# Column halves for offsets and products, and VectorE's work spread over an image's chunks, in a two-stage convolution kernel

## The reference

```python
x = x + L0(_gn(x))      # 1x1 conv 64 -> 128 channels; a 3x3 depthwise convolution whose nine taps
                        # are computed per image from the pooled hidden units by two small layers;
                        # y * tanh(softplus(y)); 1x1 conv 128 -> 64
x = x + L1(_gn(x))      # deformable 3x3 convolution, below
```

```python
offset = _conv2d(x, w_off, b_off)                       # 18 channels
mask = sigmoid(_conv2d(x, w_mask, b_mask))              # 9 channels
val = bilinear samples of x at 9 shifted points per pixel (4 corners each), times mask
xd = einsum('bikhw,oik->bohw', val, w_def)
cat = concatenate([xd, offset, mask], axis=1)
z = einsum('bihw,oi->bohw', cat, w_1x1) + b_1x1         # then a batch norm with given statistics
return silu(z)
```

## Time and profile before

| | |
|---|---|
| time, median of 3 runs (lowest to highest) | 5764.49 us (5759.78 to 5768.8) |
| the profiled execution's own time | 5764.16 us |
| its span | 5762.4 us |
| granted TensorE clock, mean | 0.833 of full speed |
| busy: TensorE matmul | 4653.8 us (81%) |
| busy: VectorE | 4582.5 us (80%) |
| busy: GpSimd | 4105.2 us (71%) |
| busy: ScalarE | 2165.7 us (38%) |
| gathers issued by GpSimd | 4308 |

### The profile page before, as it was taken

The page is one execution under the profiler, slowest core; times in us unless marked ns, Lnnn a source line. Parts: engine busy times, 40 slices in busy tenths (PEclk is TensorE's granted clock), DMA queues, the critical chain, the costliest instruction groups (busy, mean ns, idle before and its releaser), DMA issues.

```text
span 5762.4 us, 38546 instructions
## 1 busy us (share of the span) xinstructions
PE 4653.8 (81%) x11780; PEld 1745.7 (30%) x11780; DVE 4582.5 (80%) x5064; ACT 2165.7 (38%) x3057; POOL 4105.2 (71%) x4315
## 2 busy tenths in 40 slices
PE   7576888978879788787887878788897887988783
PEld 3122332323323233232332323233232332323231
DVE  5978969789696886969879697886978979688664
ACT  3333434343343433434434344343433434343320
POOL 1777677776767767677776777767777677776776
PEclk8777888978789787888988889788887888978895
DMA  3334353343534435344343443434334353433433
GB/s 97 106 121 132 99 139 109 117 131 104 142 95 131 122 106 138 94 132 118 111 136 94 132 117 114 134 98 139 109 116 130 97 146 101 129 114 106 123 108 101
DMA packets 281823, 675.11 MB, mean 117 GB/s; under 512 B 77119, under 2 KB 116618, under 8 KB 279370
## 3 DMA queue, kind: packets, MB, share of 16 engines
q0 software_dynamic: 206784, 564.93, 33.2%
q1 hardware_dynamic: 74832, 107.71, 7.4%
HBM read 618.23 MB, written 54.12 MB: 117 GB/s over the span
## 4 chain that ended last, share of the span: by engine, by line
PE 57%; DVE 28%; POOL 6%; issue 5%; ACT 2%; DMA 1%; POOLq 0%; DVEq 0%; ACTq 0%; SPq 0%
PE yo_ps L733 15%; PE z_ps L672 8%; PE conv_ps L630 7%; DVE pairs L1280 6%; DVE conv_ps L1171 6%; POOL gat L493 6%; DVE gat L1301 6%; PE yo_ps L630 5%; PE tap_ps L663 4%; PE z_ps L739 4%; PE conv_ps L553 3%; PE z_ps L671 3%; PE xh_ps L638 2%; DVE stat L1197 1%; DVE xb L1195 1%
## 5 line engine op out<-in xcount | busy, mean ns | idle before, releaser
L493 POOL DMA_INDIRECT gat<-patch_table,ixu x4308 | 4097.2, 951 | 1643.5 <-issue 1268.0
L1301 DVE TENSOR_TENSOR gat<-gat,wgt_ps 128x1024 f32<-128x1024 f32 x1077 | 1305.1, 1214 | 553.4 <-DMA gat<-patch_table,ixu 546.6
L733 PE MATMUL yo_ps<-hat_s,hat_image 128*128 128x512 f32 x3000 | 1398.0, 614 | 8.7 <-DVE hat_wy L1335 8.7
L1280 DVE TENSOR_REDUCE pairs<-gat 128x256 f32<-128x1024 f32 x1024 | 1240.2, 1211 | 0.0
L663 PE MATMUL tap_ps<-ident,pairs 128*128 128x128 f32 x2048 | 398.2, 326 | 838.1 <-DVE pairs L1280 838.1
L973 ACT ACTIVATE val<-tap_ps 128x512 f32<-128x512 f32 x512 | 304.6, 595 | 1439.2 <-PE tap_ps L663 1438.2
L733 PEld LDWEIGHTS yo_ps<-hat_s,hat_image 128*128 128x128 f32 x3000 | 562.5, 196 | 821.2 <-issue 734.5
L672 PE MATMUL z_ps<-val,w_pair 128*64 128x512 f32 x1024 | 668.0, 752 | 13.6 <-ACT val L973 13.6
L663 PEld LDWEIGHTS tap_ps<-ident,pairs 128*128 128x128 f32 x2048 | 262.1, 162 | 1217.9 <-DVE pairs L1280 1033.8
L1171 DVE SCALAR_TENSOR_TENSOR conv_ps<-xh,kb,conv_ps 128x1024 f32<-128x1024 f32 x480 | 617.8, 1287 | 12.7
L1335 DVE TENSOR_TENSOR hat_wy<-yo_ps,hat_wy 128x512 f32<-128x512 f32 x300 | 206.6, 689 | 250.7 <-PE yo_ps L733 248.0
(11 more groups left out here) (219 smaller groups left out, 4304.9 us busy)
## 6 DMA issues: line engine op xcount, KB each, us to landing
gat<-patch_table,ixu POOLq DMA_INDIRECT x4308, 2.7
xb<-in_x SPq DMA_DIRECT2D x31, 1024.0 KB, 9.7
patch_table<-rec SPq DMA_DIRECT2D x120, 256.0 KB, 2.3
hat_image<-patch_table SPq DMA_DIRECT2D x135, 128.0 KB, 4.6
out<-n_z SPq DMA_DIRECT2D x128, 128.0 KB
patch_table<-np SPq DMA_DIRECT2D x2, 1072.5 KB
patch_table<-gat SPq DMA_DIRECT2D x8, 256.0 KB, 2.2
patch_table<-rec SPq DMA_DIRECT2D x16, 97.0 KB
```

What stands on the lines that cost most here:

```text
L493: pool.indirect_dma_start(gat[:, k, t * 2 * REC:(t + 1) * 2 * REC], None, table_rows, bass.IndirectOffsetOnAxis(ixu[:, i, k, t:t + 1], 0)) ...
L733: m = pe.matmul(hat_sum[:, :], hat_image[:, i, t, :], hat_s[:, i, :], start=(i == 0), stop=(i == HI - 1))
L1280: dve.tensor_reduce(total, gat[:, k, :].rearrange("p (t x c h) -> p t c x h", t=TILES, x=2, h=2), mybir.AxisListType.XY, ALU.add).then_inc ...
L1301: dve.tensor_tensor(patch, patch, wk.rearrange("p (n h) -> p n h", h=2).unsqueeze(2).to_broadcast([128, TILES * 2, C, 2]), ALU.mult).then_ ...
```

## The change

- `has_hat`: chunks 3 and 4 of image 0 also compute their ninth tap; images 1 to 15 keep chunks 0 to 4. The table rows for it are also loaded for image 0 (`load_hat_image(0)`).
- `to_z`: every product into `z_ps` becomes two matmuls of 256 columns, the first half into partitions 0 to 63, the second into 64 to 127 of the same 256 columns of PSUM. SiLU becomes two instructions.
- `offsets_two`: the offsets of two chunks go into `om_ps`, one into partitions 0 to 40, the other into 64 to 104, alternating.
- The clip at 20 leaves VectorE: ScalarE computes relu(20 - y) and then exp(20 - that).
- `normalise` of the upper copy and the normalisation of the input in `hidden` go to ScalarE.
- `x_stats` moves from chunks 0 to 3 to chunks 5 and 6; `x_mean`, `x_var`, `x_norm`, `hidden_units`, `kernel_taps`, `kernels` from chunk 4 to chunk 7; `points` is done in two halves, for chunks 0 to 3 during chunk 6 and for chunks 4 to 7 during chunk 7; `hidden` runs at units 6 to 9 of chunk 7 instead of 4 to 7.
- `hat_post 0` moves from unit 2 to unit 3. Statistics, last row and pixels use the banks `om_ps`, `tr_ps` and `yo_ps` instead of `xh_ps`, with the waits that this asks for.

```diff
+HATS0 = (3, 4)
 HATS = (0, 1, 2, 3, 4)
-NH = len(HATS)
...
-PLAN_FIRST = ((2, "convolve 0"), (3, "convolve 1"), (5, "convolve 2"), (6, "exp"), (7, "ln"), (7, "x_stats"), (8, "tanh"))
+PLAN_FIRST = ((2, "convolve 0"), (3, "convolve 1"), (5, "convolve 2"), (6, "exp"), (7, "ln"), (8, "tanh"))
 PLAN_BLOCK0 = ((1, "project"), (3, "residual"), (3, "convolve 0"), (4, "convolve 1"), (5, "convolve 2"), (6, "exp"),
-               (7, "ln"), (7, "x_stats"), (8, "tanh"), (8, "finish"))
+               (7, "ln"), (8, "tanh"), (8, "finish"))
 PLAN_START = (
     ((2, "convolve 0"), (3, "convolve 1"), (3, "first_offsets 2"), (5, "first_offsets 3"), (5, "convolve 2"), (6, "first_pixels 1"), (6, "exp"),
-     (6, "first_offsets 4"), (7, "ln"), (7, "x_stats"), (7, "first_points 2"), (8, "tanh"), (8, "first_offsets 5"), (KK, "first_pixels 2")),
+     (6, "first_offsets 4"), (7, "ln"), (7, "first_points 2"), (8, "tanh"), (8, "first_offsets 5"), (KK, "first_pixels 2")),
     ((1, "project"), (3, "residual"), (3, "convolve 0"), (3, "first_offsets 6"), (4, "convolve 1"), (4, "first_offsets 7"), (5, "first_pixels 3"),
-     (5, "convolve 2"), (6, "exp"), (6, "first_points 3"), (7, "ln"), (7, "x_stats"), (8, "tanh"), (8, "finish")),
+     (5, "convolve 2"), (6, "exp"), (6, "first_points 3"), (7, "ln"), (8, "tanh"), (8, "finish")),
     ((1, "project"), (3, "residual"), (3, "convolve 0"), (4, "convolve 1"), (5, "convolve 2"), (6, "exp"), (6, "first_points 4"),
-     (7, "ln"), (7, "x_stats"), (8, "tanh"), (8, "finish")),
+     (7, "ln"), (8, "tanh"), (8, "finish")),
 )
-PLAN_NORM = ((1, "project"), (3, "residual"), (4, "x_mean"), (4, "group_mean"), (5, "x_var"), (6, "group_var"), (6, "x_norm"),
-             (7, "hidden_units"), (8, "kernel_taps"), (8, "finish"), (8, "normalise"), (KK, "kernels"))
+PLAN_NORM = ((1, "project"), (3, "residual"), (4, "group_mean"), (5, "group_var"), (6, "normalise"), (8, "finish"))
 PLAN_PREPARE = (
-    ((1, "last_row"), (1, "to_table 0"), (2, "offsets 0"), (3, "to_table 1"), (3, "offsets 1"),
-     (4, "to_table 2"), (5, "to_pixels 0"), (5, "to_table 3"), (6, "offsets 2"),
-     (7, "offsets 3"), (8, "to_table 4"), (8, "finish"), (KK, "to_pixels 1")),
-    ((1, "offsets 4"), (2, "offsets 5"), (2, "to_table 5"), (3, "to_pixels 2"), (4, "offsets 6"), (4, "to_table 6"),
-     (5, "offsets 7"), (6, "to_table 7"), (7, "to_pixels 3"), (8, "finish")),
-    ((1, "points 0"), (2, "points 1"), (2, "next_indices"), (3, "points 2"), (4, "hidden 0"), (5, "hidden 1"),
-     (6, "hidden 2"), (7, "hidden 3"), (8, "finish")),
+    ((1, "last_row"), (1, "offsets 0"), (2, "to_table 0"), (2, "x_stats 0"), (3, "to_table 1"), (4, "offsets 1"), (4, "to_pixels 0"),
+     (5, "to_table 2"), (5, "x_stats 1"), (6, "to_table 3"), (7, "to_pixels 1"), (8, "to_table 4"), (8, "finish")),
+    ((1, "offsets 2"), (2, "to_table 5"), (2, "points 0"), (3, "offsets 3"), (3, "to_pixels 2"), (4, "points 1"), (4, "to_table 6"),
+     (5, "x_stats 2"), (5, "to_table 7"), (6, "points 2"), (6, "to_pixels 3"), (7, "x_stats 3"), (8, "finish")),
+    ((1, "x_mean"), (1, "points 3"), (2, "x_var"), (2, "points 4"), (2, "next_indices"), (3, "x_norm"), (3, "points 5"),
+     (4, "hidden_units"), (5, "kernel_taps"), (6, "kernels"), (6, "hidden 0"), (7, "hidden 1"), (8, "hidden 2"), (8, "finish"), (KK, "hidden 3")),
 )
-PLAN_HAT = ((1, "hat_rows"), (1, "hat_up 0"), (2, "hat_post 0"), (3, "hat_up 1"), (5, "hat_post 1"), (5, "hat_out 0"), (5, "hat_up 2"),
+PLAN_HAT = ((1, "hat_rows"), (1, "hat_up 0"), (3, "hat_post 0"), (3, "hat_up 1"), (5, "hat_post 1"), (5, "hat_out 0"), (5, "hat_up 2"),
             (6, "hat_out 1"), (7, "hat_post 2"), (7, "hat_up 3"), (8, "hat_out 2"), (KK, "hat_post 3"))
 PLAN_NEXT_HAT = ((1, "hat_y"), (3, "hat_part"), (4, "hat_x"), (6, "hat_mask"), (8, "hat_weigh"), (KK, "hat_select"))
 
 
 def has_hat(q):
 
-    return NCH <= q < B * NCH and q % NCH in HATS
+    return q < B * NCH and q % NCH in (HATS if q >= NCH else HATS0)
...
+        def row_ps(n):
+
+            return xh_ps if n == 0 else tr_ps
+
+        def stat_ps(n):
+
+            return xh_ps if n == 0 else om_ps
+
+        def pixel_ps(n):
+
+            return xh_ps if n == 0 else yo_ps
...
+            load_hat_image(0)
...
+                if n > 1:
+                    pe.wait_ge(rec_done, n * NCH + 1)
                 pe.matmul(steps_ps(n)[:, MEAN:MEAN + 1], pair2[C:, :], aggr0[C:, 0:1], start=True, stop=True).then_inc(kernel_pe, 1)
...
+                    if n > 1 and s == 0 and j == 0:
+                        pe.wait_ge(kernel_dve, n * KERNEL_STEPS + 8)
...
+            def offsets_two(n, s):
+
+                if s == 0:
+                    pe.wait_ge(np_done, n * 2 + 2)
+                else:
+                    pe.wait_ge(om_done, n * NCH + s * 2)
+                for i in range(6):
+                    for j in range(2):
+                        m = pe.matmul(om_ps[C * j:C * j + OM, :], w_om[:, i, :], inner(np1, 0, 128, (s * 2 + j) * ROWS + 2 * (i // 3), i % 3),
+                                      start=(i == 0), stop=(i == 5))
+                m.then_inc(om_mm, 2)
...
                 pe.wait_ge(om_done, n * NCH + s * 2 + 2)
+                if n > 0 and ups[0]:
+                    pe.wait_ge(hat_scaled, ups[0])
+                if n > 0:
+                    after_px.append(n * NCH + s * 2 + 3)
...
+            def to_z(weights, columns, start=False, stop=False):
+
+                for j in range(2):
+                    m = pe.matmul(z_ps[C * j:C * j + C, 0:CH // 2], weights, columns[:, j * CH // 2:(j + 1) * CH // 2], start=start, stop=stop)
+                return m
+
             def product(q, p):
 
                 pe.wait_ge(tap_done, copies_before(q) + p + 3)
                 if p == 0:
                     rows = slice(side(q // NCH), side(q // NCH) + OM)
-                    pe.matmul(z_ps[0:C, :], w_cat[rows, :], cat[rows, span(q % NCH)], start=True, stop=False)
-                pe.matmul(z_ps[0:C, :], w_pair[:, p, :], val[:, p % 2, :], start=False, stop=False)
+                    to_z(w_cat[rows, :], cat[rows, span(q % NCH)], start=True)
+                to_z(w_pair[:, p, :], val[:, p % 2, :])
 
             def last_products(b, g):
 
                 q = b * NCH + g
                 if not has_hat(q):
                     pe.wait_ge(tap_done, copies_before(q) + COPIES + 2)
-                    pe.matmul(z_ps[0:C, :], w_single, val[0:C, PAIRS % 2, :], start=False, stop=True).then_inc(z_mm, 1)
+                    to_z(w_single, val[0:C, PAIRS % 2, :], stop=True).then_inc(z_mm, 1)
                 else:
                     pe.wait_ge(hat_scaled, HT * hats_before(q) + HT)
-                    pe.matmul(z_ps[0:C, :], w_hat[:, :], hat_wy[:, HT - 1, :], start=False, stop=True).then_inc(z_mm, 1)
+                    to_z(w_hat[:, :], hat_wy[:, HT - 1, :], stop=True).then_inc(z_mm, 1)
 
             def sample(b, g, lo=0, hi=KK):
...
+                if after_px:
+                    pe.wait_ge(px_done, after_px.pop())
+                ups[0] = HT * h + t + 1
...
+                if n > 1:
+                    if s == 0:
+                        act.wait_ge(kernel_dve, n * KERNEL_STEPS + 7)
+                    for j in range(2):
+                        act.wait_ge(xh_mm, n * NCH + s * 2 + (j + 1))
+                        act.activation(n0[C:, j, :], xb[C:, n % 2, span(s * 2 + j)], ACT.Identity, bias=mr0[C:, 2:3],
+                                       scale=mr0[C:, 1:2]).then_inc(n0_done, 1)
...
+                    twenty = hat_c[:, HI + HT + 3:HI + HT + 4]
+                    if n == 1 and s == 0:
+                        act.wait_ge(hat_consts, ALL_HAT)
+                    act.wait_ge(conv_sum, (n - 1) * CONV_SUMS + s * KK + KK)
+                    act.activation(u[:, :, :].rearrange("p j c -> p (j c)"), conv2_ps[:, :], ACT.Relu, bias=twenty, scale=-1.0).then_inc(clip, 2)
                     act.wait_ge(clip, n * NCH + s * 2 + 2)
-                    act.activation(u[:, :, :].rearrange("p j c -> p (j c)"), u[:, :, :].rearrange("p j c -> p (j c)"), ACT.Exp).then_inc(exp_done, 2)
+                    act.activation(u[:, :, :].rearrange("p j c -> p (j c)"), u[:, :, :].rearrange("p j c -> p (j c)"), ACT.Exp, bias=twenty,
+                                   scale=-1.0).then_inc(exp_done, 2)
...
+                if n > 0:
+                    act.activation(np1[0:C, 1:1 + H, 1:1 + W], xb[0:C, n % 2, :].rearrange("p (r w) -> p r w", w=W),
+                                   ACT.Identity, bias=nmean1[0:C, :], scale=rinv1[0:C, :]).then_inc(np_done, 1)
...
+            def offsets_two(n, s):
+
+                for j in range(2):
+                    offsets(n, s * 2 + j, j)
+
...
-                act.activation(zs[:, :], z_ps[0:C, :], ACT.Silu, bias=bn_shift[:, :], scale=bn_scale[:, :]).then_inc(zs_done, 1)
+                for j in range(2):
```

(16 more changed lines are left out.)

97 lines of the change are left out of this document (50 added, 47 removed).

## The result

The changed kernel takes 5571.24 us (median, 5558.37 to 5586.32) beside 5762.14 us for the kernel before: a ratio of 0.967 [0.9646, 0.9693], 3.3% faster. The forecast was 5543; 5571 lies inside the range, 28 us above it. The profiled execution took 5569.03 us, its span is 5567.2 us, its mean granted clock 0.779 (0.833 before).

The account below looks back on a forecast made before the run. GpSimd's gathers were taken as the bound: first gather 119.15, 4299 gathers at 1.257 (5403.8), tail 14.0, 1.8 over the span and 4 for stalls gave 5543 us; range 5510 to 5665.

Parts of the forecast that it names:

- The sum: Whole run: first gather 119.15, gathers 5403.8, tail 14.0, 1.8 over the span, 4 for stalls in image 0: 5543 us.
- the leads: Time from GpSimd's first gather of a chunk to VectorE's start of it: 4.5, 9.3, 14.1, 18.9 at chunks 1 to 4.
- Chunk 7 in 45.2, lead 4.5 at chunk 0: Chunk 7: VectorE busy 35 us in 45.2, pixel wait of 9.52 gone, GpSimd 4.5 us ahead at the next chunk 0.
- the limit: Chunks 1 to 3: GpSimd more than 21.8 us ahead of VectorE stalls, waiting for transposes of taps not yet summed.
- Chunk lengths: Chunk 0 falls from 41.9 to 39.3 us, 1 to 3 from 47.6 to 45.0, 4 to about 33; 5 to 7 take 45.2.
- the 2.6 us per chunk: VectorE in chunks 0 to 3 loses the clip (1.23) and two statistics (2 x 0.68): 2.6 us.
- charged at nothing: Moved `hat_post 0`: no gain; TensorE starts `hat_up 1` some 4 us later, next needed at `hat_post 1`, unit 5.
- No part of my sum rests on the halves: Column halves on TensorE may save 4.1 us per chunk with a computed tap, 22 per image on offsets; none counted.
- Chunk 7 stays long: Rival, chance 0.09: chunk 7 lasts 61.35 us as before, stalls 8.4 us per image in 14 images: 5660 us.
- Halves one after the other: Rival, chance 0.06: TensorE's halves do not overlap, 5.7 us more in chunks 0 to 4: also about 5660 us.
- Clock: Rival, chance 0.05: TensorE's granted clock falls in chunks 0 to 4 and TensorE bounds them; at 0.58, 6090 us.
- The signs: `tap_ps` waits near zero, chunks 0 to 4 about 40 us, VectorE waiting in 5, 6, 7, 0; wrong if gathers exceed 1.27.

Follow-up runs that it names:

- a_hats4: The changed kernel with the ninth tap of chunk 4 gathered again in images 1 to 15 (60 gathers more): ratio 0.9747 to the kernel before.
- a_xstats: The changed kernel with the input statistics back in chunks 0 to 3, at unit 7: ratio 0.9669 to the kernel before.
- a_clip: The changed kernel with the clip at 20 back on VectorE, ScalarE's relu pass gone: ratio 0.9882 to the kernel before.

## Why the prediction was right, and where it was off

- **What bounds the kernel.** Right. Over 14 runs a gather costs 1.254 to 1.259 us, and what moves the span is stalls, 24 to 485 us. Taking TensorE and VectorE work away makes the changed kernel slower (a_hats4). In the kernel before, with TensorE's 57% of the chain, no run takes TensorE work away; there the reading rests on the sum of gathers and stalls.
- **The sum.** 26 us short of the profiled time: stalls 24 instead of 4 (+20), a gather 1.2587 instead of 1.257 (+7), a tail of 12.7 instead of 14.0 (-1).
- **The step that was mis-sized: the leads.** "Chunk 7 in 45.2, lead 4.5 at chunk 0" measured 55.0 and 14.3. VectorE's work in it was right, 35.23 for 35; the time around it wasn't: `hat_select` and the wait of 4.01 for SiLU stand at its end. Leads at chunks 3 and 4 were 25.3 and 29.6 for the forecast 14.1 and 18.9. That cost little, 1.6 us of stalls per image, because the limit had risen too, from 21.8 to 24.4: the transposes of taps 4 and 5 come 2.6 us sooner in the changed chunks, and the prediction took the old times. It had 7.7 us of room under the limit; there were none. That the range held owes something to luck: with whole products, or with the clip on VectorE, the stalls are back (71 and 182 us).
- **Chunk lengths.** 1 to 3: forecast 45.0, measured 45.3, 44.5, 44.6. Chunk 0: 41.8 for 39.3. Chunk 4: 31.6 for 33. Chunk 5: 30.4 for 45, since VectorE was still catching up there.
- **Right by luck: the 2.6 us per chunk.** The two statistics (1.36) are worth nothing (a_xstats); the clip (1.23) is worth 1.8 to 3.1, its own time and what `hat_up 2` loses at the low clock. The sum came out nearly the same.
- **`hat_post 0`, "charged at nothing".** Wrong: 1.9% in the changed kernel, 0.9% alone. I priced TensorE's delay, which is real and free, and not VectorE's wait at the old place, which is what goes in the changed kernel (chunks 0 to 3 are 1.0 to 3.0 us longer with it).
- **"No part of my sum rests on the halves."** Wrong, 1.2%: without them leads pass 30 and stalls are 126 us.
- **Rivals.** Chunk 7 stays long: no, though 55 is over my 53. Halves one after the other: no. The rule of the Trainium skill that I weighed (page "TensorE: Matmul & The Clock Gate", section "Part 3: Packing small matmuls") lets a weight load overlap only between different row groups; the trace disagrees for these column halves, 24 instructions in the time of 12. The same section gives 2.38x for three column tiles of 32. The trace agrees in kind: two halves bring 2.0x on the offsets, and 1.7x on the products (one every 1.00 us before, every 0.58 us after, at the full clock). Clock: the mean did fall, 0.833 to 0.779, but in chunks 6 and 7 (0.69, 0.50), where TensorE has time; chunks 0 to 4 kept 0.85 to 0.94. So the rival as I wrote it didn't come, but the clock does count inside a chunk, as a_clip shows.
- **The signs.** Waits for `tap_ps` near zero: 42 us, of which 24 are stalls. Chunks 0 to 4 at about 40: 42 to 45, then 32. A gather over 1.27: no. VectorE waiting for gathers in chunks 5, 6, 7 and 0: yes.

## What to carry to other kernels

When one engine streams in order and the others only hold it up now and then, write the span as its count times its price plus its stalls, and judge every edit by the stalls. Here the lead has a limit: below it an edit is worth nothing, over it each us counts, and a delay ahead of a chain can cost more than its own time, so parts tested alone (0.2%, 0.9%) and parts taken away (1.2, 2.1, 1.9%) don't add up to the whole. A large wait on an engine with time to spare can be the good side of a trade; look at what the engine with the work waits for. And when an edit is worth nothing, look at what else the next step waits for: the clip moved alone freed an engine that TensorE wasn't waiting for.

## What the runs showed of the hardware

- Two fp32 matmuls that write different column halves (outputs in partitions 0 to 40 and 64 to 104) and read the same rows run fully side by side when they alternate, weight loads included: 5.35 us for 24, 5.31 for 12, and 8.82 for 24 that don't alternate.
- The ten instructions of a `hat_up` take 4.56 us at a granted clock of 1.00 and 7.30 at 0.62.
- The price of a gather differs a little from run to run, 1.2537 to 1.2587 us, without a link to the edits that I could find; over 4300 that is 22 us, about the spread of the changed kernel's times (28 us).

What stays open: the parts that were never taken away alone, above all the points in two halves, the small steps moved from chunk 4 to 7 and the two normalisations on ScalarE. Chunk 4 is 6.5 us shorter, and no tested part accounts for more than 2.1 of it; that the moved steps do is read from the plan and the traces, not shown by a run. The lead at chunk 0 is 6.8 us shorter: without the halves it is back at 20.2, and `hat_post 0` alone brings it to 15.3, so what the split of the points adds to these can't be told. Open too is why the clock is low in part of `hat_up 2` in a_clip and not in the changed kernel, and whether computed taps in chunk 5 pay once the offsets there are spread out, which wasn't tried.
